# The state-space stage's output by chunks of 128 tokens, with C repeated from ScalarE's queue and every part's slot moved

## The reference, cut to what matters

```python
zxbcdt = einsum('bld,ed->ble', rmsnorm(x), W_in)      # z, xBC, dt
xBC = silu(conv4(xBC)); xs, Bm, Cm = split(xBC)
dt = softplus(dt + dt_bias); dA = exp(dt * -exp(A_log))
state = state * dA_t + (dt_t * x_t) * B_t             # 1024 steps, 8 heads, 32 x 32
y = state . C_t + Dp * xs
y = rmsnorm(y * silu(z), gnorm_w)
return x + einsum('ble,de->bld', y, W_out)
```

## Time and profile before

| | us |
|---|---|
| median of 3 runs | 1116.74 (1116.7 to 1120.18) |
| the profiled execution, its own time | 1116.23 |
| its span, first to last instruction | 1114.4 |
| attention stage and the part that runs once | to 364 |
| scan | 364 to about 849 |
| experts | from about 849 |

### The profile page before, as it was taken

How to read it: one execution, slowest core, us unless ns; L and a number is a source line. 1 busy time by engine, 2 the same in 40 slices (tenths; PEclk the granted TensorE clock), 3 DMA queues, 4 the chain that set the end, 5 groups by cost and what they waited for, 6 DMA issues and landing times.

```text
span 1114.4 us, 20011 instructions
## 1 busy us (share of the span) xinstructions
PE 928.4 (83%) x7790; PEld 737.3 (66%) x7790; DVE 712.2 (64%) x1838; ACT 542.2 (49%) x859; POOL 236.8 (21%) x194
## 2 busy tenths in 40 slices
PE   3798899988986786878787797778979999999998
PEld 2554665556655575766676676667757878888877
DVE  2856776777662746364646446564566888878875
ACT  1534554444744653628273454626334455655453
POOL 0052001110104241414223141412532001111000
PEclk8899999999986778788878778787959999999999
DMA  5420000000002200203030200303010000000000
GB/s 148 153 114 19 19 20 2 19 20 20 1 9 57 49 19 15 52 2 65 1 67 1 47 20 8 60 1 66 7 53 1 20 1 20 20 20 20 20 1 39
DMA packets 30765, 36.16 MB, mean 32 GB/s; under 512 B 4560, under 2 KB 24784, under 8 KB 30672
## 3 DMA queue, kind: packets, MB, share of 16 engines
q1 hardware_dynamic: 29520, 30.68, 11.3%
q10 hardware_dynamic: 1152, 4.19, 1.0%
HBM read 21.50 MB, written 4.98 MB: 24 GB/s over the span
## 4 chain that ended last, share of the span: by engine, by line
PE 53%; DVE 28%; ACT 8%; issue 6%; POOL 2%; DMA 1%; SPq 1%; DVEq 0%; ACTq 0%; POOLq 0%
PE ps L1028 6%; DVE cacc L1682 6%; PE ps L684 5%; PE ps L947 4%; PE ps L763 3%; DVE acc L1959 3%; PE ps L765 3%; PE ps L764 3%; PE ps L671 3%; DVE nmax L1539 2%; PE ps L638 2%; ACT X L1234 2%; ACT un L1354 2%; PE ps L883 2%; PE ps L643 2%
## 5 line engine op out<-in xcount | busy, mean ns | idle before, releaser
L1773 DVE SCALAR_TENSOR_TENSOR dcy<-dcy,g_sb 128x1024 f32<-128x1024 f32 x64 | 95.4, 1491 | 117.9 <-ACT dcy L1310 117.5
L1959 DVE SCALAR_TENSOR_TENSOR acc<-ps,comb,acc 128x128 f32<-128x128 f32 x512 | 141.2, 344 | 21.5 <-PE ps L1028 20.6
L1028 PEld LDWEIGHTS ps<-w_f,hid 128*128 128x128 f32 x1024 | 131.2, 191 | 16.5 <-ACT hid L1373 8.2
L1028 PE MATMUL ps<-w_f,hid 128*128 128x128 f32 x1024 | 136.7, 277 | 4.8 <-ACT hid L1373 4.8
L1373 ACT ACTIVATE hid<-ps,b_f 128x512 f32<-128x512 f32 x128 | 86.3, 686 | 107.7 <-PE ps L765 107.4
L1310 ACT ACTIVATE dcy<-ps 128x1024 f32<-128x1024 f32 x64 | 65.4, 1021 | 134.9 <-PE ps L883 134.8
L1539 DVE TENSOR_REDUCE nmax<-ps 128x1 f32<-128x1024 f32 x64 | 78.1, 1221 | 39.7 <-PE ps L643 39.3
L518 POOL TENSOR_TENSOR xdt<-xs,dts 128x256 f32<-128x256 f32 x64 | 58.3, 913 | 211.6 <-PE ps L924 211.6
L1682 DVE SCALAR_TENSOR_TENSOR cacc<-ps,cw,cacc 128x1023 f32<-128x1023 f32 (+5 forms) x72 | 91.8, 1276 | 8.6 <-ACT cacc L1247 7.2
L1163 ACT ACTIVATE probs<-ps,nmax 128x1024 f32<-128x1024 f32 x64 | 71.3, 1114 | 41.3 <-DVE nmax L1539 38.4
L671 PEld LDWEIGHTS ps<-id_f,probs 128*128 128x128 f32 x512 | 60.0, 144 | 32.5 <-issue 22.9
(11 more groups left out here) (212 smaller groups left out, 1990.3 us busy)
## 6 DMA issues: line engine op xcount, KB each, us to landing
c_dec<-exp_dram SPq DMA_DIRECT2D x32, 256.0 KB, 5.1
xc<-in_x SPq DMA_DIRECT2D x8, 512.0 KB, 3.3
q_b<-q_a SPq DMA_DIRECT2D x16, 256.0 KB, 2.8
X<-in_x_tok ACTq DMA_DIRECT2D x8, 512.0 KB, 5.3
c_rep<-cacc SPq DMA_DIRECT2D x32, 128.0 KB, 2.4
out<-o_ch SPq DMA_DIRECT2D x8, 512.0 KB, 2.6
w_f<-in_w SPq DMA_DIRECT2D x2, 512.0 KB, 4.3
cst_f<-in_sel_rows SPq DMA_DIRECT2D x1, 512.0 KB, 5.8
```

The costliest lines, as they stand in the source:

```text
L1028: last = nc.tensor.matmul(ps[:, Y_BANKS[n], t * P:(t + 1) * P], hid[n % 2][:, t * P:(t + 1) * P], w2_f[:, e, :], start=True, stop=True)
L1773: nc.vector.scalar_tensor_tensor(mix[c % 2][:], dcy[c % 2][:], 1.0, g_sb[u][:, c:c + 1, :].to_broadcast([P, NH, P]), ALU.min, ALU.mult).th ...
L1959: done = nc.vector.scalar_tensor_tensor(acc[u][:, tt, :], ps[:, bank, t * P:(t + 1) * P], comb[u][:, tt, e:e + 1], acc[u][:, tt, :], ALU.m ...
```

## The change: what it does

- The output projection and the sum of squares go by chunk: n = 8b + c numbers the chunks through all pictures. In chunk n PE sums the squares of chunk n - 2 and multiplies its rows by `w_out` into columns 384 to 511 of bank 6 or 7, ahead of chunk n's output rows. DVE takes the mean of that one column behind gating chunk n, POOL takes one root, and DVE scales and adds the tile in chunk n + 1. The wait for the convolution ahead of the old `out_product` is gone. Banks 2 and 3 are no longer used for it.
- `increments` waits for the chunk before to be gated and for chunk n - 3 to be added, as both use bank 7.
- `gates` for column group 1 goes first, at slot 0, ahead of the first chunk's output rows, behind a wait for all three convolutions of its picture; group 0 stays at slot 0.5. ACT takes the two z groups in that order.
- `silus` moves from slot 1.5 to slot 1, which is ahead of `square(b, 0)`, and ends with the waits and the four transfers into `c_rep`, now on ACT's queue. SP has them no more.
- `normed` moves from 3.5 to 2, `high` from 4.5 to 3.75, `shortcut` from 0.5 to 4, the parts of the picture two ahead earlier by half a slot on PE, ACT and DVE, mostly. `group` 0 stands at 4.5, before `decay(6)`.
- On POOL `decayed` and `weighted` are cut in two pieces each, one piece at slots 3.5, 4.5, 5.5 and 6.5.
- In the part that runs once, `inner_products(0, 0)` goes behind `steps(1, 1)` and picture 1's first group, on DVE `inner` behind `low` and `steps`.
- Behind the scan only the last two chunks' outputs are left on PE, and three on DVE.

```diff
-                sp.wait_ge(m_silu_ready, 3 * b + 3)
...
-                for h in range(4):
-                    sp.dma_start(c_rep[h * DS:(h + 1) * DS], cacc[b % 3][DS:2 * DS, 2, :]).then_inc(m_c_spread, 16)
...
+            pool_parts = [(totals, (), 3.5), (decayed, (0,), 3.5), (decayed, (1,), 4.5), (weighted, (0,), 5.5),
+                          (weighted, (1,), 6.5)]
...
-                    beside(b, u, first, last, c)
+                    n = NT * b + c
                     if c + 1 < NT:
                         operand(b, u, c + 1)
-                    beside(b, u, first, last, c + 0.5)
+                    if n >= 2:
+                        root(n - 2)
+                    pieces(b, c + 0.5)
+                    if first and c == 2:
+                        norms(B - 1)
...
-                    elif b == 0:
-                        pe.wait_ge(m_conv_ready, 2)
-                    elif b == 1:
-                        pe.wait_ge(m_conv_ready, 6)
                     else:
-                        pe.wait_ge(m_x_updated, b - 1)
+                        pe.wait_ge(m_conv_ready, 3 * b + (3 if b > 0 else 2))
...
-            def sum_of_squares(b, c):
-                pe.wait_ge(m_square_ready, NT * b + c + 1)
+            def sum_of_squares(n):
+                pe.wait_ge(m_square_ready, n + 1)
                 for g in range(2):
-                    last = nc.tensor.matmul(ps[:, 6 + c % 2, DI + c // 2:DI + c // 2 + 1], sqt[:, c % 4, g, :], ones_f[:, 0:1],
+                    nc.tensor.matmul(ps[:, 6 + n % 2, DI:DI + 1], sqt[:, n % 4, g, :], ones_f[:, 0:1],
+                                     start=(g == 0), stop=(g == 1))
...
+            def out_product(n):
+                t = slice(n % NT * P, (n % NT + 1) * P)
+                for g in range(2):
+                    last = nc.tensor.matmul(ps[:, 6 + n % 2, BANK - P:BANK], y_t[:, g, t], w_out[:, g, :],
                                             start=(g == 0), stop=(g == 1))
-                if c == NT - 1:
-                    last.then_inc(m_squares_summed, 1)
...
-            def out_product(b):
...
-                pe.wait_ge(m_gated_ready, NT * b + NT)
-                if b + 2 < B:
-                    pe.wait_ge(m_conv_ready, 3 * (b + 2) + 3)
-                else:
-                    pe.wait_ge(m_inner_ready, B)
...
+                return last
...
+                    n = NT * b + c
                     if c == 0:
                         decay(b, u, 0, first)
-                        if not first:
-                            pe.wait_ge(m_gated_ready, NT * b)
-                            sum_of_squares(b - 1, NT - 2)
-                            sum_of_squares(b - 1, NT - 1)
-                            out_product(b - 1)
                     pieces(b, c - 0.25)
                     if c + 1 < NT:
                         decay(b, u, c + 1)
                     pieces(b, c)
-                    if c == 0 and not first:
-                        pe.wait_ge(m_square_mean_ready, b)
-                    if c >= 2 or not first:
-                        pe.wait_ge(m_gated_ready, NT * b + c - 1)
-                    if c >= 2:
-                        sum_of_squares(b, c - 2)
+                    if c == 1:
+                        pe.wait_ge(m_state_ready, b + 1)
+                    if n >= 4:
+                        pe.wait_ge(m_out_added, n - 3)
+                    if n >= 2:
+                        pe.wait_ge(m_gated_ready, n - 1)
+                        sum_of_squares(n - 2)
+                        out_product(n - 2)
                     output_rows(b, u, c)
                     if c == 0:
+                        if n > 0:
+                            pe.wait_ge(m_gated_ready, n)
+                            pe.wait_ge(m_out_added, n - 2)
                         increments(b, u)
                     pieces(b, c + 0.5)
...
+            pe_parts = [(cumulate, (), 1, -0.25), (gates, (1, 0), 1, 0), (gates, (1, 1), 1, 0), (gates, (0, 0), 1, 0.5),
+                        (gates, (0, 1), 1, 0.5), (turn_x, (0,), 1, 2.5), (turn_x, (1,), 1, 2.5), (turn_b, (), 1, 3),
+                        (inner_products, (), 1, 3), (turn_normed, (), 2, 3.5), (steps, (), 2, 4.5),
+                        (group, (0, 0), 2, 4.5), (group, (0, 1), 2, 4.5), (group, (1, 0), 2, 5),
+                        (group, (1, 1), 2, 5), (group, (2, 0), 2, 6), (group, (2, 1), 2, 6)]
...
-            inner_products(0, 0)
             steps(1, 1)
             for g in range(3):
                 for h in range(2):
                     group(1, 1, g, h)
+                if g == 0:
+                    inner_products(0, 0)
...
-            pe.wait_ge(m_gated_ready, NT * B)
-            sum_of_squares(B - 1, NT - 2)
-            sum_of_squares(B - 1, NT - 1)
-            pe.wait_ge(e_gates_copied, 1)
-            out_product(B - 1)
+            for n in (NT * B - 2, NT * B - 1):
+                pe.wait_ge(m_gated_ready, n + 1)
+                pe.wait_ge(m_out_added, n - 1)
+                sum_of_squares(n)
+                out_product(n).then_inc(m_tail_product, 1)
...
-                for g in range(2):
-                    act.wait_ge(m_z_product, 3 * b + 2 + g)
+                for g in (1, 0):
+                    act.wait_ge(m_z_product, 3 * b + 3 - g)
...
                 nc.scalar.preload_act_table_set("natural_log_exp_and_others")
+                act.wait_ge(m_silu_ready, 3 * b + 3)
+                act.sem_inc(wait_carrier, 1)
+                if b > 0:
+                    act.wait_ge(m_c_decayed, 2 * b)
+                    act.sem_inc(wait_carrier, 1)
+                    act.wait_ge(m_inner_product, b)
+                    act.sem_inc(wait_carrier, 1)
+                for h in range(4):
+                    nc.scalar.dma_start(c_rep[h * DS:(h + 1) * DS], cacc[b % 3][DS:2 * DS, 2, :]).then_inc(m_c_spread, 16)
...
+            act_parts = [(factors, (), 1, 0), (silus, (), 1, 1), (normed, (), 2, 2), (gather_x, (), 1, 2.75),
+                         (gather_b, (), 1, 3), (high, (), 2, 3.75), (shortcut, (), 1, 4), (steps, (), 2, 4.75),
+                         (tap, (0,), 2, 4.75), (tap, (1,), 2, 5.5), (softplus, (), 2, 5.5), (tap, (2,), 2, 6.5)]
...
+            dve_parts = [("exponents", (), 1, -0.25), ("ends", (), 1, 1), ("inner", (), 1, 3.5), ("low", (), 2, 4),
+                         ("steps", (), 2, 5), ("conv", (0, 1), 2, 5), ("conv", (0, 2), 2, 5.5),
+                         ("conv", (0, 3), 2, 5.75), ("conv", (1, 1), 2, 6), ("softplus", (0,), 2, 6),
+                         ("softplus", (1,), 2, 6), ("conv", (1, 2), 2, 6.5), ("conv", (1, 3), 2, 6.75),
+                         ("conv", (2, 1), 2, 7), ("conv", (2, 2), 2, 7.5), ("conv", (2, 3), 2, 7.5)]
...
+            def mean_square(n):
+                if n >= 4:
+                    dve.wait_ge(m_rms_ready, n - 3)
+                nc.vector.tensor_scalar(sve[:, n % 4:n % 4 + 1], ps[:, 6 + n % 2, DI:DI + 1], 1.0 / DI, GN2_EPS, ALU.mult,
...
+            def output(n):
...
+                b, c = n // NT, n % NT
+                dve.wait_ge(m_rms_ready, n + 1)
+                if c == 0:
+                    dve.wait_ge(m_residual_ready, b + 1)
+                xb = X[:, b, c * P:(c + 1) * P]
+                nc.vector.scalar_tensor_tensor(xb, ps[:, 6 + n % 2, BANK - P:BANK], srs[:, n % 4:n % 4 + 1], xb,
+                                               ALU.mult, ALU.add).then_inc(m_out_added, 1)
...
                     if c < NT - 1:
                         mixed(b, u, c + 1)
-                    if c == 1 and not first:
-                        output(b - 1, 1 - u)
+                    n = NT * b + c
+                    if n >= 3:
+                        output(n - 3)
...
                     dve.wait_ge(m_y_product, NT * b + c + 1)
                     dve.wait_ge(m_z_ready, 2 * b + 2)
-                    if c == 0 and not first:
-                        dve.wait_ge(m_out_product, b)
                     r = slice(c * P, (c + 1) * P)
                     nc.vector.tensor_tensor(y_t[:, :, r], ps[:, 6 + c % 2, 0:DI].rearrange("p (g t) -> p g t", g=2),
                                             zs[u][:, :, r], ALU.mult).then_inc(m_gated_ready, 1)
+                    if n >= 2:
+                        mean_square(n - 2)
...
-            fronts[0]["inner"]()
             fronts[1]["low"]()
             fronts[1]["steps"]()
+            fronts[0]["inner"]()
...
-            mean_square(B - 1)
-            output(B - 1, 1)
+            output(NT * B - 3)
+            for n in (NT * B - 2, NT * B - 1):
+                dve.wait_ge(m_tail_product, n - NT * B + 3)
+                mean_square(n)
+                output(n)
```

More of the change, by code:

```diff
@@ L519, in operand, with totals @@
                                         ALU.mult).then_inc(m_xdt_ready, 1)
-            def decayed(b, u):
+            def totals(b, u):
                 pool.wait_ge(m_row_factors_spread, 64 * (b + 1))
@@ L531, in decayed, with weighted @@
```

(39 more changed lines are left out.)

80 lines of the change are left out of this document (19 added, 61 removed).

## The result

The changed kernel takes 1138.7 us at the median (1136.18 to 1140.86), the kernel before 1116.7 in the same comparison: the ratio is 1.0195, with a 95% interval of 1.0154 to 1.0235. So the change costs 1.5 to 2.4%. The profiled execution took 1136.18 us, with a span of 1134.2: 19.8 us over the span before.

What follows compares the result with a forecast made beforehand. PE was taken to mostly set the end, not alone. Five pictures +18.0, picture 0 +4, pictures 6 and 7 +1, start -3.5, end -2.5: +17 on 1116.2 gives 1133 us; own range 1122 to 1144, 8-in-10 range 1098 to 1153.

Steps and rivals of the forecast that it cites:

- pictures 1 to 5 +18: Five pictures inside the scan, each forecast 3.6 us longer, +18.0 us in sum.
- picture 0 +4: First picture: the stall and the issues cost without the output product's gain, +4 us, between 0 and +8.
- pictures 6 and 7 +1: Last two pictures: POOL's pieces of decayed and weighted spread over four chunks, +1 us for both.
- start -3.5: Ahead of the scan: B-C products now beside the transfers, less ACT's issues, -3.5 us, between -1 and -6.
- end -2.5: Behind the scan: root, adds and products leave the path, a second mean, root and add come: -2.5 us.
- 66 to 68: Sign that the forecast is right: a picture's period of 66 to 68 us; under 63 us would be wrong.
- A wait of PE in chunk 2: Sign: about 8 us before the sum of squares, released by ACT's square, once in each of pictures 1 to 6.
- +2.4 to `steps`: From the last convolution's end to the first steps matmul: start at 41.6 us instead of 39.2, 2.4 us later.
- the first rival: Full clock comes back soon behind the chunk 2 stall: -1.7 us a picture, 1100.7 us in all; chance 0.28.
- +1.2 behind `steps`: From steps to the last convolution: earlier first convolution against 3 us more DVE work, +1.2 us, between -1 and +3.
- 2.9 at the gates: PE from the last convolution's end through gates to chunk 1's exponential: about 10 us instead of 12.9, gain 2.9.
- The four issues: C transfers issued from ACT's queue behind silus: 1.6 to 2.3 us of ACT a picture, taken as 2.2.

Runs made afterwards that it cites:

- e1: Changed kernel with ACT's silus moved from slot 1 to 1.5, behind square(b, 0): 1149.3 us, 1.0312 of the kernel before.
- e7: Output by chunks, POOL's cut and new start of the changed kernel; PE, ACT, DVE slots of the kernel before, C transfers on SP: 1085.1 us, 0.9747.
- e10: e7 plus the changed kernel's later slots (inner_products 3, turn_normed 3.5, steps and group 0 at 4.5, groups at 5 and 6): 1118.2 us, 1.0017.
- e11: e7 plus the changed kernel's early slots (gates of group 1 at 0, silus 1, normed 2, inner_products 3), later slots old: 1123.0 us, 1.0070.
- e8: Changed kernel with silus behind square(b, 0), C transfers on SP, normed at 0.5 and low at 3.75, ahead of mixed(5): 1085.7 us, 0.9729.
- e9: e7 plus the four C transfers issued by ACT instead of SP: 1124.5 us, 1.0060 of the kernel before.

## Why the prediction was right, and where it was not

The total was right: 1133 forecast, 1138.7 measured, inside the forecast's own range, and slower. Its parts were not, and made up for each other, so that the total came out so near is luck: pictures 1 to 5 +18 against +4.6, picture 0 +4 (0 to 8) against +12.4, pictures 6 and 7 +1 against +5.6 for picture 6; start -3.5 against -2.0, end -2.5 against -0.8 with picture 7. The period was 64.9 us, and not one of 66 to 68.

**Confirmed.** A wait of PE in chunk 2 once a picture, released by ACT's square, 7.3 us against 8; behind it the low clock; a gap of ACT behind the second table load, 10.6 us in seven pictures, so 1.5 each against the 2.2 taken, just under the bounds of 1.6 to 2.3; no wait ahead of a long product; the root at 0.56 us against 0.5.

**The term "+2.4 to `steps`".** Measured from the prediction's mark, the end of the last convolution, `steps` begin 38.6 us behind it in the kernel before and 38.2 in the changed one (means over pictures 1 to 5): -0.4, and in picture 3 36.6 for 39.3. The gates of group 1 took 1.5 us at the full clock, and not 2.8. In picture 3, from the end of the last convolution (574.6), ACT began its silus at 7.8, not at 10, and the stall ended at 17.1, not at 20.3. The clock came back within it: `turn_x` ended at 23.9, not at 28.5. This was the first rival's mechanism. The rule cited there, that sustained work brings the clock back ("TensorE: Matmul & The Clock Gate", section "Part 1: The HAM clock gate" in the Trainium skill), agrees with the changed kernel's two windows and not with e1's ten busy microseconds at 0.51. From the scan to `steps` the loss is 3.9 us all the same, as the scan itself comes 4.3 us sooner behind the convolution (10.3 us before, 6.0 now).

**The term "+1.2 behind `steps`" and the 2.9 at the gates.** From `steps` to the last convolution the changed kernel takes 27.1 us for 25.2: +1.9, inside the bounds of -1 to +3. The output by chunks was under-priced, with 2.9 us up to chunk 1. Alone (e7) it saves 5.5 us a picture, and 5.3 of them between the last convolution and `steps` (33.3 us for 38.6): the scan comes 5.2 us behind the convolution, for 10.3, and the rest of the way is as long as before. Of 38.0 us of waits that went, I had carried over only a part. The new tail, which I took as good for 1 to 3 us at DVE's first convolution, is part of e10, which loses 33 us against e7. That the tail costs by itself is not shown, since e11 with the old tail is as slow from `steps` to the scan (33.5 us) and e8 with the new one is not (30.9).

**The four issues.** Sized at 2.2 us a picture beside a path, they cost 1.5 of ACT's time, and 6.1 a picture on top of e7 (e9). Within the full change they are worth 5 to 10 us in all, and nothing in pictures 1 to 5 of the profiles. What the Trainium skill says ("DMA: Bandwidth & Descriptors", section "Issuing engines are not separate DMA queues"), that the time to issue is usually small beside the transfer, does not hold here: ACT stood still for 1.47 and 1.53 us, and a transfer landed 2.4 us behind its issue. The estimate of 0.2 us for ACT was far too low, and the Trainium skill gives its dispatch of about 50 ns, in the same page's section "Anatomy of one DMA — SWDGE (gpsimd) path", for a DMA that GpSimd issues, and not for ACT. In these rows ACT also passes the semaphore waits ahead of the issues, and no run parts the two.

**Picture 0.** I gave it the stall and the issues. It also has `steps` and the first group's products at half clock behind the wait for `xl`, ahead of decay(7) on PE, so that DVE waits 8.19 us for one exponential (6.21 in picture 3):

```profile
412.32 0.38 PE L800 MATMUL ps<-w_dt,xh 128*128 128x16 f32 x1 [2.83 <-DVE xl L1661]
```

```profile
420.85 1.22 DVE L1761 SCALAR_TENSOR_TENSOR dcy<-dcy,g_sb 128x1024 f32<-128x1024 f32 x1 [8.19 <-ACT dcy L1298]
```

Of its 12.4 us, 6.1 lie before `steps` and 6.3 behind. With the old slots and C on SP (e7) the picture takes 64.7 us, less than the 66.8 before. That the clock is what separates these stretches is read from equal work at two durations; no run could set the clock by itself. Why PE's clock is at 0.77 in e10, with only 0.8 us more of idle time a picture than in e7, is not settled either.

## What to carry to other kernels

Price a wait of the matrix engine with what the clock does behind it: the same four issues cost nothing in a picture of the changed kernel, 1.4 to 2.2 us in three other pairs and 6.1 in the one that ran well (e9), so parts of a change must be tried one by one and not summed. When a stall is found, look at who stands next in the releaser's queue before moving it: with the square ahead, PE simply waited for the copies behind it. A change that is slower in total can hold a part that is worth 2.5%. And a forecast of the total is a weak test of its parts: measure each term from the mark that it was set up with.

## What was not expected of the hardware

Two waits of 3.7 and 3.5 us with little work between them were followed by 10.1 us at 0.51 of the clock under a PE that was busy throughout; one of 7.3 us was followed by 0.64 over 6.5 us. Four transfers issued from ACT held it for 1.47 to 1.53 us, and the queue for 2.45. A root of one column took 559 ns on POOL, against 1650 for eight.
